# Routed experts on one core: the gathered rows of every second unit turned by VectorE from quarter rows, in place of four TensorE transposes

## The chip, the core and the metric

The kernel runs on one core of one Trainium2 chip. The metric is the time of the whole kernel in microseconds (us), less is better. Everything between the first load and the last store is in it.

## The reference, cut to what matters

The input `x` is 4 x 512 tokens of 512 numbers. A cross attention and a self attention (16 heads) are added to it; then comes the part that matters here, a mixture of 16 experts, six of which each token goes through:

```python
t = rmsnorm(x, ln2_w).reshape(-1, d)              # T = 2048 tokens, d = 512
probs = softmax(t @ gate_w.T)                      # E = 16 experts
topv, topi = top_k(probs, 6); topv = topv / sum(topv)
cw = zeros((T, E)).at[arange(T)[:, None], topi].add(topv)
g = einsum('td,eid->eti', t, eg_w)                 # I = 352
u = einsum('td,eid->eti', t, eu_w)
routed = einsum('eti,edi,te->td', silu(g) * u, ed_w, cw)
shared = silu(t @ sg_w.T) * (t @ su_w.T) @ sd_w.T
out = x + routed + shared
```

All is in fp32. A product of two fp32 matrices is made of three matmuls on parts (`matmul3`: high x high, high x low, low x high), where the high part is the number cut to the type fp32r and the low part is what is left.

## The kernel before, in words

The program is a chain of blocks: cross attention, self attention (beside it GpSimd splits all expert weights into high and low parts and stores them in memory), the second normalization, the shared expert with the routing tables, and last `routed_experts`, which the change is about.

The routing tables sort the (token, expert) pairs by expert and fill units of 128 lanes; there are `UNITS` = 111 units, whatever the routing. For each unit, `token_of[:, n]` has the 128 token numbers, `weight_of[:, n]` their weights; `expert_of` and `base_of` tell TensorE which expert it is and where its weights lie in the ring. The normalized rows lie in memory as `rows` (T + 128 rows of 512 numbers, 2 KB each; the last 128 are spare, for empty lanes).

What is done for a unit n, by engine (q = n % 2 chooses the buffer):

- GpSimd gathers the 128 rows of the unit into `xg[q]` by an indirect DMA (L1616), indexed by `gidx[q]`, which VectorE has copied from `token_of` (L1773). Later it scatters the unit's result `y[q]` with an add into the output (L1620). A scatter waits until the one before it has landed (semaphore `added`), because two of them may meet in one row. Before each of the two, a small instruction on `carry` (L1627) takes the waits. In its step m GpSimd issues the gather of unit m + 2 and the scatter of unit m - 3.
- TensorE transposes the gathered rows into `ps_x[q]` in four 128x128 transposes (`transposed`, L1664), ScalarE copies them out as the high part `xT[q][0]` (L1729), VectorE makes the low part (`low_rows`, L1754).
- TensorE makes the gate and the up product (`gate_up`, 24 matmuls of 352 columns, lines 67 to 69), ScalarE the silu (L1734), VectorE the product `prod` (L1767); TensorE transposes `prod` (`products`, L1697), ScalarE and VectorE split it into `hT` (L1738, L1775); TensorE makes the down product (`down`, 9 matmuls of 512 columns); VectorE weighs it into `y[q]` (`weigh`, L1762).

The order on each engine is written out by hand, in `step`; loops (`Fori`) run over pairs of units. TensorE's step n is: transposes of the rows of unit n + 2, register loads (`base`, `expert`), transposes of `prod` of unit n, gate and up product of unit n + 1, down product of unit n. VectorE's step n is: `prod` of n, `y` of n - 1, low part of the rows of n + 2, index copy for n + 4, `hT` low part of n. SyncE loads the weights of the experts into a ring of three slots, 16 pieces of 272 KB each (L1610), when the expert that had the slot is done.

Each engine waits with semaphores that count finished instructions: `pe_x` for the row transposes, `act_x` and `dve_x` for the copies, `dve_i` for the index copies, `ld_x` for the gathers. Here are `routed_experts` and what calls it:

Of the kernel before, what the change touches and what calls it, by code (L numbers as in the profile page):

```python
# [619 lines left out]
def routed_counters(sem):  # L620

    counters, count = counting(sem)
    for name in ("pool_c5", "pe_x", "act_x", "dve_x", "pe_g5", "pe_u5", "act_s5", "dve_p5", "pe_h5", "act_h5", "dve_h5",
                 "pe_d5", "dve_y", "dve_i"):
        count(name)
    return counters
# [939 lines left out]
def routed_experts(nc, sem, counters, ps, ident, token_of, weight_of, expert_of, base_of, ends_of, rows, ring, xg, ld_x, ld_ring,  # L1566
# [15 lines left out]
    with ExitStack() as ctx:  # L1582
# [10 lines left out]
        ps_g, ps_u, ps_x, ps_h, ps_d = ps[0], ps[1], ps[2:4], ps[4], ps[5:7]  # L1593

        pool_0 = sem("pool_05")
        (pool_c, pe_x, act_x, dve_x, pe_g, pe_u, act_s, dve_p, pe_h, act_h, dve_h, pe_d, dve_y, dve_i) = counters
# [16 lines left out]
        @block.gpsimd  # L1613
        def _(pool):
            def gather(q):
                nc.gpsimd.indirect_dma_start(xg[q][:, 0, :], None, rows, bass.IndirectOffsetOnAxis(ap=gidx[q][:], axis=0),  # L1616
                                             bounds_check=T + P - 1, oob_is_err=True).then_inc(ld_x[q], 16)

            def scatter(q):
                nc.gpsimd.indirect_dma_start(out, bass.IndirectOffsetOnAxis(ap=sidx[q][:], axis=0), y[q][:], None,  # L1620
                                             bounds_check=T + P - 1, oob_is_err=True,
                                             compute_op=ALU.add).then_inc(added, 16)

            def take_waits(done):
# [4 lines left out]
            def step(m, q, scatters=True, gathers=True):  # L1629

                if gathers:
                    pool.wait_ge(dve_i, ONE + m - 1)
                    pool.wait_ge(pe_x, ONE + m + 1)
                    take_waits(2 * m - 4)
                    gather(q)
                if scatters:
                    pool.wait_ge(dve_y, ONE + m - 2)
                    pool.wait_ge(added, FIRST + 16 * (m - 3))
                if gathers:
                    take_waits(2 * m - 3)  # L1640
                if scatters:
                    scatter(1 - q)

            nc.gpsimd.memset(carry[:], 0.0).then_inc(pool_0, 1)
            nc.gpsimd.memset(prod[:, I:NI * P], 0.0).then_inc(pool_0, 1)
            pool.wait_ge(pool_0, 2)
            pool.wait_ge(added, FIRST)
            for m in range(2, 4):
                if m == 3:
                    pool.wait_ge(stored, STORED)  # L1650
                step(m, m % 2, scatters=m > 2)
            with pool.Fori(2, TURNS + 1) as g:
                for q in range(2):
                    step(2 * g + q, q)
            for m in range(2 * TURNS + 2, UNITS + 3):
                step(m, m % 2, gathers=m + 2 < UNITS)
            pool.wait_ge(added, FIRST + 16 * UNITS)

        @block.tensor
        def _(pe):  # L1660
            def transposed(landed, q, half=0):
                pe.wait_ge(ld_x[q], 16 * landed)
                for j in range(DC):
                    last = nc.tensor.transpose(ps_x[q][:, j * P:(j + 1) * P], xg[q][:, half, j * P:(j + 1) * P], ident[:])  # L1664
                last.then_inc(pe_x, 1)

# [33 lines left out]
            def step(n, turn, q, half=0, rows=True, following=True, weighed=True):  # L1700
# [13 lines left out]
            gate_up(first, its_expert, 0, 0)  # L1714
            pe.wait_ge(pool_0, 2)
            for n in range(2):
                step(n, 0, n, half=1, weighed=False)
            with pe.Fori(1, TURNS + 1) as g:
                for q in range(2):
                    step(2 * g + q, g, q)  # L1720
            for n in range(2 * TURNS + 2, UNITS):
                step(n, n // 2, n % 2, rows=n + 2 < UNITS, following=n + 1 < UNITS)

        @block.scalar
        def _(act):
            def high_rows(n, q):

                act.wait_ge(pe_x, ONE + n + 1)
                nc.scalar.copy(xT[q][0][:], ps_x[q][:].rearrange("p (j t) -> p j t", j=DC)).then_inc(act_x, 1)  # L1729

            def step(n, q, more=True):
                act.wait_ge(pe_g, ONE + n + 1)
                act.wait_ge(dve_p, ONE + n)
                nc.scalar.activation(silu[:], ps_g[:, 0:I], ACT.Silu).then_inc(act_s, 1)  # L1734
                if more:
                    high_rows(n + 2, q)
                act.wait_ge(pe_h, ONE + n + 1)
                nc.scalar.copy(hT[0][:], ps_h[:, 0:NI * P].rearrange("p (c t) -> p c t", c=NI)).then_inc(act_h, 1)  # L1738

            for q in range(2):  # L1740
                high_rows(q, q)
            for n in range(2):
                step(n, n)
            with act.Fori(1, TURNS + 1) as g:
                for q in range(2):
                    step(2 * g + q, q)
            for n in range(2 * TURNS + 2, UNITS):
                step(n, n % 2, more=n + 2 < UNITS)

        @block.vector  # L1750
        def _(dve):
            def low_rows(n, q):
                dve.wait_ge(act_x, ONE + n + 1)
                nc.vector.tensor_tensor(xT[q][1][:], ps_x[q][:].rearrange("p (j t) -> p j t", j=DC),  # L1754
                                        xT[q][0][:].bitcast(F32), ALU.subtract).then_inc(dve_x, 1)
# [8 lines left out]
            def step(n, q, before=True, gathers=True, more=True):  # L1764
# [7 lines left out]
                if gathers:  # L1772
                    nc.vector.tensor_copy(gidx[q][:], token_of[:, bass.ds(n + 4, 1)]).then_inc(dve_i, 1)  # L1773
# [4 lines left out]
            dve.wait_ge(added, FIRST)  # L1778
            for q in range(2):
                low_rows(q, q)  # L1780
            for n in range(2):
                step(n, n, before=n > 0)
            with dve.Fori(1, TURNS) as g:
                for q in range(2):
                    step(2 * g + q, q)
            for n in range(2 * TURNS, UNITS):
                step(n, n % 2, gathers=n + 4 < UNITS, more=n + 2 < UNITS)
# [102 lines left out]
```

## Time and profile before

Three runs took 2204.24, 2204.88 and 2204.95 us, a median of 2204.88.

| what | value |
|---|---|
| profiled execution, its own time | 2203.29 us |
| its span, first to last instruction | 2201.4 us |
| PE (TensorE matmul) busy | 2122.8 us, 96% |
| DVE (VectorE) busy | 1145.1 us, 52% |
| POOL (GpSimd) busy | 962.9 us, 44% |
| ACT (ScalarE) busy | 720.7 us, 33% |
| mean granted TensorE clock | 0.987 of 2.4 GHz |
| DMA, mean over the span | 137 GB/s |
| routed stage | from about 1438 us to the end |

Times in the rows are in microseconds from the start of the span, unless they are marked ns. PEld is TensorE's weight load, which lies beside its matmuls. An engine's busy time leaves out register, branch and semaphore instructions. In a bracket behind a row stands how long the engine was idle before it and what released it; "issue" is idle time in which nothing that the profile shows was waited for. The time of a POOL DMA instruction is that in which GpSimd writes the descriptors; the data lands later.

### The profile page before, as it was taken

The numbers are of one execution on the slowest core, as the hardware profiler recorded it, in microseconds if no ns is written. First come the engines' busy times: TensorE is split into PE (matmuls) and PEld (weight loads), VectorE is DVE, ScalarE is ACT, GpSimd is POOL, SyncE is SP. The second block draws the span as 40 slices with busy tenths as digits, with TensorE's granted clock in tenths as the row PEclk, the third lists the DMA queues.
The fourth block names the chain that finished last, engine by engine and source line by source line (L and its number), as shares of the span: only waits on it lengthen the run. The fifth ranks groups of instructions, "written<-read, shape, count | busy, mean of one in ns | idle before, by whom it ended". The sixth has DMA issues, their size and how long they took to land. (4 is left out here: it accounts for less than half of the span.)

```text
span 2201.4 us, 39664 instructions
## 1 busy us (share of the span) xinstructions
PE 2122.8 (96%) x11850; PEld 1856.1 (84%) x11851; DVE 1145.1 (52%) x2520; ACT 720.7 (33%) x1896; POOL 962.9 (44%) x1004
## 2 busy tenths in 40 slices
PE   7899999999999999999996999989999999999996
PEld 6788888889888898888875777789999999999996
DVE  6746466464655646465666476633433333333332
ACT  6634344343434434343344222212222222222221
POOL 3545354545545454554515014434444444444442
PEclk9999999999999999999997999999999999999998
DMA  3214343443533344343416111186766766676443
GB/s 116 86 68 168 120 144 117 157 143 115 170 120 138 123 151 154 114 162 118 150 62 225 77 67 48 45 256 159 226 172 179 194 186 160 159 216 185 81 76 53
DMA packets 140690, 300.62 MB, mean 137 GB/s; under 512 B 16800, under 2 KB 16800, under 8 KB 138592
## 3 DMA queue, kind: packets, MB, share of 16 engines
q1 hardware_dynamic: 115392, 241.26, 31.0%
q0 software_dynamic: 24960, 58.21, 14.0%
q8 instruction: 27, 0.44, 0.1%
q10 hardware_dynamic: 288, 0.53, 0.1%
q14 instruction: 23, 0.19, 0.0%
HBM read 177.51 MB, written 122.42 MB: 136 GB/s over the span
## 5 line engine op out<-in xcount | busy, mean ns | idle before, releaser
L726 POOL TENSOR_TENSOR chunk_hi<-chunk_raw,zero 128x512 fp32r<-128x512 f32 x153 | 159.4, 1042 | 241.2 <-DMA chunk_raw<-in_whole 241.2
L1620 POOL DMA_INDIRECT out<-y,sidx x111 | 177.4, 1598 | 66.1 <-issue 44.4
L728 POOL TENSOR_TENSOR chunk_raw<-chunk_raw,chunk_hi 128x512 fp32r<-128x512 f32 x153 | 197.7, 1292 | 12.0
L936 DVE TENSOR_TENSOR pT_lo<-ps,pT_hi 128x384 fp32r<-128x384 f32 (+2 forms) x256 | 111.1, 455 | 176.6 <-ACT pT_hi L878 172.6
L1767 DVE TENSOR_TENSOR prod<-ps,silu 128x352 f32<-128x352 f32 x111 | 58.2, 524 | 271.0 <-PE ps L69 271.0
L909 DVE SCALAR_TENSOR_TENSOR HS<-ps,rinv,HS 128x512 f32<-128x512 f32 x260 | 176.6, 738 | 3.3 <-PE ps L69 3.3
L1627 POOL TENSOR_TENSOR carry<-ident 128x1 f32<-128x1 f32 x214 | 41.5, 194 | 295.9 <-DVE gidx L1773 209.6
L867 ACT ACTIVATE prob<-ps,negmax 128x512 f32<-128x512 f32 (+3 forms) x256 | 131.6, 527 | 110.0 <-DVE negmax L898 110.0
L1762 DVE TENSOR_SCALAR y<-ps,weight_of 128x512 f32<-128x512 f32 x111 | 83.3, 750 | 140.8 <-PE ps L69 140.7
L67 PE MATMUL ps<-ring,xT_0hi 128*128 x448 | 150.0, 335 | 0.8 <-DMA ring<-split_weights 0.8
L67 PE MATMUL ps<-wv_or_qk_hi,hT_hi 128*128 128x256 f32 x512 | 146.8, 287 | 2.9 <-PEq L134 2.9
L67 PE MATMUL ps<-ring,xT_1hi 128*128 x440 | 146.7, 333 | 0.0
L68 PE MATMUL ps<-wv_or_qk_lo,hT_hi 128*128 128x256 f32 x512 | 146.0, 285 | 0.0
L69 PE MATMUL ps<-wv_or_qk_hi,hT_lo 128*128 128x256 f32 x512 | 146.0, 285 | 0.0
L69 PE MATMUL ps<-ring,xT_0lo 128*128 x448 | 144.1, 322 | 0.0
L68 PE MATMUL ps<-ring,xT_0hi 128*128 x448 | 144.1, 322 | 0.0
L69 PE MATMUL ps<-ring,xT_1lo 128*128 x440 | 142.6, 324 | 0.0
L68 PE MATMUL ps<-ring,xT_1hi 128*128 x440 | 141.5, 322 | 0.0
L1616 POOL DMA_INDIRECT xg<-normed_rows,gidx x107 | 114.9, 1074 | 57.5 <-issue 36.7
L69 PE MATMUL ps<-ring,hT_lo 128*128 x333 | 131.4, 395 | 0.0
L67 PE MATMUL ps<-ring,hT_hi 128*128 x333 | 129.8, 390 | 1.4 <-DVE hT_lo L1775 1.4
L68 PE MATMUL ps<-ring,hT_hi 128*128 x333 | 131.1, 394 | 0.0
(322 smaller groups left out, 6002.1 us busy)
## 6 DMA issues: line engine op xcount, KB each, us to landing
ring<-split_weights SPq DMA_DIRECT2D x240, 272.0 KB, 6.8
chunk_raw<-in_whole SPq DMA_DIRECT2D x153, 256.0 KB, 2.7
split_weights<-chunk_hi SPq DMA_DIRECT2D x153, 256.0 KB, 2.4
split_weights<-chunk_raw SPq DMA_DIRECT2D x153, 256.0 KB, 2.6
xg<-in_wqk SPq DMA_DIRECT2D x16, 512.0 KB, 3.8
x_spill<-x SPq DMA_DIRECT2D x4, 1024.0 KB, 3.9
xg<-in_wv SPq DMA_DIRECT2D x8, 512.0 KB, 3.5
xg<-in_wo SPq DMA_DIRECT2D x8, 512.0 KB, 5.1
```

Source lines behind the costliest of these rows:

```text
L67: nc.tensor.matmul(out, lhs[0], rhs[0], start=start, stop=False)
L68: nc.tensor.matmul(out, lhs[0], rhs[1], start=False, stop=False)
L69: return nc.tensor.matmul(out, lhs[1], rhs[0], start=False, stop=stop)
L726: nc.gpsimd.tensor_tensor(chunk_hi[k][:], chunk_raw[k][:], zero[:].to_broadcast([P, CH]), ALU.add).then_inc(chunk_high, 1)
L728: nc.gpsimd.tensor_tensor(chunk_raw[k][:].bitcast(F32R), chunk_raw[k][:], chunk_hi[k][:].bitcast(F32), ALU.subtract).then_inc(chunk_low, 1)
L867: nc.scalar.activation(prob[i][:], ps_s[i][:, 0:(i + 1) * P], ACT.Exp, bias=negmax[:, s % 2, i:i + 1], accum_out=rsum[:, s % 2, i:i + 1]). ...
L909: nc.vector.scalar_tensor_tensor(out=hs, in0=ps_w[i][:], scalar=rinv[:, (s - 1) % 2, i:i + 1], in1=hs, op0=ALU.mult, op1=ALU.add).then_inc ...
L936: nc.vector.tensor_tensor(pT[1][:, 0:split, w], ps_t[k % 2][:, 0:split * P].rearrange("p (j t) -> p j t", t=P), pT[0][:, 0:split, w].bitca ...
L1616: nc.gpsimd.indirect_dma_start(xg[q][:, 0, :], None, rows, bass.IndirectOffsetOnAxis(ap=gidx[q][:], axis=0), bounds_check=T + P - 1, oob_i ...
L1620: nc.gpsimd.indirect_dma_start(out, bass.IndirectOffsetOnAxis(ap=sidx[q][:], axis=0), y[q][:], None, bounds_check=T + P - 1, oob_is_err=Tr ...
L1762: nc.vector.tensor_scalar(y[q][:], ps_d[q][:], weight_of[:, bass.ds(n, 1)], None, ALU.mult).then_inc(dve_y, 1)
L1767: nc.vector.tensor_tensor(prod[:, 0:I], ps_u[:, 0:I], silu[:], ALU.mult).then_inc(dve_p, 1)
```

## The change

Units 5, 7, ... 109 (odd, from the fifth on) get their transposed rows in another way. The transpose on VectorE turns each block of 32x32 in its place. So GpSimd gathers quarter rows, of 512 bytes: partition 32a + j gets, for t = 0 to 3, the quarter a of the row of lane 32t + j. These are four indirect DMAs of 128 quarter rows each, in place of one of 128 rows. Then one VectorE transpose of 128x512 from `xg[1]` (which it reads with a step of four elements) into `ps_x[1]` gives the turned rows. The indices of the quarters, `quarter_of` = 4 x token + a, are made once, at the stage's start, by four small fp32 matmuls on TensorE that spread the token numbers over the partitions and one VectorE instruction; ScalarE makes the operands of these matmuls.

With that the order of the 512 features over chunk and partition becomes (partition, chunk) in place of (chunk, partition), for all units and the experts' gate and up weights; the host lays out the weights so, and TensorE's transposes that are left read `xg` with a step of four elements. TensorE's step of an odd unit has no row transposes any more; its register loads are made ahead of the last chunk of the down product before it. ScalarE's and VectorE's copies out of `ps_x` have the same number of elements in another order. VectorE's turn for the rows of unit n + 2 stands first in its step n, and GpSimd may gather into `xg[1]` again when the turn is done (`dve_turned`).

```diff
-        gidx = [sb(f"gidx{q}", [P, 1], U32) for q in range(2)]
+        gidx = [sb(f"gidx{q}", [P, 1 + 3 * q], U32) for q in range(2)]
+        tokens = sb("tokens5", [P, UNITS])
+        lanes = sb("lanes5", [P, 4, P])
+        group = sb("group5", [P, 1])
+        quarter_of = sb("quarter_of", [P, UNITS, 4], U32)
...
+        quarters = rows.rearrange("r (a n) -> (r a) n", a=4)
...
+        turned_rows = lambda q: [ps_x[0][:].rearrange("p (c t j) -> p t c j", c=DC, t=4),
+                                 ps_x[1][:].rearrange("p (t c j) -> p t c j", t=4, c=DC)][q]
+        of_parts = lambda x: x[:].rearrange("p c (t j) -> p t c j", t=4)
...
             def gather(q):
-                nc.gpsimd.indirect_dma_start(xg[q][:, 0, :], None, rows, bass.IndirectOffsetOnAxis(ap=gidx[q][:], axis=0),
-                                             bounds_check=T + P - 1, oob_is_err=True).then_inc(ld_x[q], 16)
+                if q == 0:
+                    nc.gpsimd.indirect_dma_start(xg[0][:, 0, :], None, rows, bass.IndirectOffsetOnAxis(ap=gidx[0][:], axis=0),
+                                                 bounds_check=T + P - 1, oob_is_err=True).then_inc(ld_x[0], 16)
+                    return
+                for t in range(4):
+                    nc.gpsimd.indirect_dma_start(xg[1][:, 0, t * P:(t + 1) * P], None, quarters,
+                                                 bass.IndirectOffsetOnAxis(ap=gidx[1][:, t:t + 1], axis=0),
+                                                 bounds_check=4 * (T + P) - 1, oob_is_err=True).then_inc(ld_x[1], 16)
...
                 if gathers:
                     pool.wait_ge(dve_i, ONE + m - 1)
-                    pool.wait_ge(pe_x, ONE + m + 1)
+                    if m < 4:
+                        pool.wait_ge(pe_x, ONE + m + 1)
+                    elif q == 0:
+                        pool.wait_ge(pe_x, ONE + turn + 3)
+                    else:
+                        pool.wait_ge(dve_turned, ONE + turn - 1)
                     take_waits(2 * m - 4)
                     gather(q)
                 if scatters:
...
             def transposed(landed, q, half=0):
                 pe.wait_ge(ld_x[q], 16 * landed)
-                for j in range(DC):
-                    last = nc.tensor.transpose(ps_x[q][:, j * P:(j + 1) * P], xg[q][:, half, j * P:(j + 1) * P], ident[:])
+                by_tile = xg[q][:, half, :].rearrange("p (m c) -> p c m", c=DC)
+                for c in range(DC):
+                    last = nc.tensor.transpose(ps_x[q][:, c * P:(c + 1) * P], by_tile[:, c], ident[:])
                 last.then_inc(pe_x, 1)
+            def token_quarters():
+                pe.wait_ge(act_tokens, 2)
+                for t in range(4):
+                    last = nc.tensor.matmul(ps_q[:, t * UNITS:(t + 1) * UNITS], lanes[:, t, :], tokens[:], start=True, stop=True)
+                last.then_inc(pe_tokens, 1)
...
-            def down(at, n, q, weighed=True):
+            def down(at, n, q, weighed=True, between=None):
                 if weighed:
                     pe.wait_ge(dve_y, ONE + n - 1)
                 pe.wait_ge(dve_h, ONE + n + 1)
+                found = None
                 for c in range(NI):
+                    if between and c == NI - 1:
+                        found = between()
                     last = matmul3(nc, ps_d[q][:], [h[:, c, :] for h in hT], weights(at, GU + c * D, D), c == 0, c == NI - 1)
                 last.then_inc(pe_d, 1)
+                return found
...
+            def places(n, following=True):
+                return (base(n), base(n + 1), expert(n + 1)) if following else (base(n),)
+            def step(n, turn, q, half=0, rows=True, following=True, weighed=True, found=None, between=None):
                 if rows:
                     transposed(turn + 2, q, half)
-                own = base(n)
-                if following:
-                    at, its_expert = base(n + 1), expert(n + 1)
+                own, *after = found or places(n, following)
                 products(n)
                 if following:
-                    gate_up(at, its_expert, n + 1, 1 - q)
-                down(own, n, q, weighed)
+                    gate_up(*after, n + 1, 1 - q)
+                return down(own, n, q, weighed, between)
...
+            token_quarters()
             pe.wait_ge(pool_0, 2)
             for n in range(2):
                 step(n, 0, n, half=1, weighed=False)
             with pe.Fori(1, TURNS + 1) as g:
-                for q in range(2):
-                    step(2 * g + q, g, q)
+                found = step(2 * g, g, 0, between=lambda: places(2 * g + 1))
+                step(2 * g + 1, g, 1, rows=False, found=found)
             for n in range(2 * TURNS + 2, UNITS):
-                step(n, n // 2, n % 2, rows=n + 2 < UNITS, following=n + 1 < UNITS)
+                step(n, n // 2, n % 2, rows=n % 2 == 0 and n + 2 < UNITS, following=n + 1 < UNITS)
...
+            def high_rows(n, turn, q):
+                if n < 4:
+                    act.wait_ge(pe_x, ONE + n + 1)
+                    nc.scalar.copy(xT[q][0][:], ps_x[q][:].rearrange("p (j t) -> p j t", j=DC)).then_inc(act_x, 1)
+                    return
+                if q == 0:
+                    act.wait_ge(pe_x, ONE + turn + 3)
+                else:
+                    act.wait_ge(dve_turned, ONE + turn - 1)
+                    act.wait_ge(pe_u, ONE + n - 1)
+                nc.scalar.copy(of_parts(xT[q][0]), turned_rows(q)).then_inc(act_x, 1)
...
+            nc.scalar.copy(tokens[:], token_of[:]).then_inc(act_tokens, 1)
+            nc.scalar.copy(lanes[:].rearrange("p t (a j) -> p t a j", a=4),
+                           ident[:].rearrange("p (t j) -> p t j", t=4).unsqueeze(2).to_broadcast([P, 4, 4, 32])).then_inc(act_tokens, 1)
...
+            def turn_rows(n, turn):
+                dve.wait_ge(ld_x[1], 32 + 64 * (turn - 1))
+                dve.wait_ge(act_x, ONE + n - 1)
+                dve.wait_ge(dve_x, ONE + n - 1)
+                nc.vector.transpose(ps_x[1][:].rearrange("p (t c j) -> p t c j", t=4, c=DC),
+                                    xg[1][:, 0, :].rearrange("p (t i c) -> p t c i", t=4, c=DC)).then_inc(dve_turned, 1)
...
+            def step(n, turn, q, before=True, gathers=True, more=True):
+                if q and more and n >= 2:
+                    turn_rows(n + 2, turn + 1)
                 dve.wait_ge(act_s, ONE + n + 1)
                 dve.wait_ge(pe_u, ONE + n + 1)
                 nc.vector.tensor_tensor(prod[:, 0:I], ps_u[:, 0:I], silu[:], ALU.mult).then_inc(dve_p, 1)
...
                 if more:
                     low_rows(n + 2, q)
                 if gathers:
-                    nc.vector.tensor_copy(gidx[q][:], token_of[:, bass.ds(n + 4, 1)]).then_inc(dve_i, 1)
+                    if q == 0:
+                        nc.vector.tensor_copy(gidx[0][:], token_of[:, bass.ds(n + 4, 1)]).then_inc(dve_i, 1)
+                    else:
+                        nc.vector.tensor_copy(gidx[1][:], quarter_of[:, bass.ds(n + 4, 1), :].rearrange("p u t -> p (u t)")).then_inc(dve_i, 1)
...
+            for a in range(4):
+                nc.vector.memset(group[32 * a:32 * a + 32, :], float(a)).then_inc(dve_quarters, 1)
             for q in range(2):
                 low_rows(q, q)
+            dve.wait_ge(dve_quarters, 4)
+            dve.wait_ge(pe_tokens, 1)
+            nc.vector.tensor_scalar(quarter_of[:].rearrange("p u t -> p t u"),
+                                    ps_q[:, 0:4 * UNITS].rearrange("p (t u) -> p t u", t=4), 4.0, group[:, 0:1],
+                                    ALU.mult, ALU.add).then_inc(dve_quarters, 1)
+            dve.wait_ge(dve_quarters, 5)
...
-    gu = gu.transpose(0, 1, 3, 2).reshape(NE, 2, DC, P, I).transpose(3, 0, 1, 2, 4).reshape(P, NE, GU)
+    gu = gu.transpose(0, 1, 3, 2).reshape(NE, 2, P, DC, I).transpose(2, 0, 1, 3, 4).reshape(P, NE, GU)
```

## Rows read from the trace of the kernel before

**Rows 1.** One stretch: length; busy PE, PEld, DVE, ACT, POOL; clock, DMA share, GB/s

```profile
1450.00:1700.00 250.00, 250.00 (x1496) 233.68 (x1496) 96.28 (x224) 53.27 (x112) 113.09 (x150) 1.00 0.71 187
```

**Rows 2.** TensorE in order of time, two units (start, duration, x count)

```profile
1600.39 0.39 PE L69 MATMUL ps<-ring,hT_lo 128*128 x1
...
1607.05 0.39 PE L69 MATMUL ps<-ring,hT_lo 128*128 x1
1607.28 0.60 PE L1664 MATMUL ps<-ident,xg 128*128 128x128 f32 x4
1607.71 0.49 PE L1697 MATMUL ps<-ident,prod 128*128 128x128 f32 x3
...
1613.76 0.39 PE L69 MATMUL ps<-ring,hT_lo 128*128 x1
```

**Rows 3.** GpSimd in order of time where it is behind

```profile
1641.64 1.60 POOL L1620 DMA_INDIRECT out<-y,sidx  x1 [0.58 <-issue]
...
1643.71 1.08 POOL L1616 DMA_INDIRECT xg<-normed_rows,gidx  x1 [0.24 <-issue]
1646.58 0.19 POOL L1627 TENSOR_TENSOR carry<-ident 128x1 f32<-128x1 f32 x1 [1.79 <-DMA out<-y,sidx]
1647.43 1.60 POOL L1620 DMA_INDIRECT out<-y,sidx  x1 [0.66 <-issue]
```

**Rows 4.** instructions of L1616, then of L1620: issue to landing

```profile
DMA to landing us min/median/max: 3.3/3.5/7.4
DMA to landing us min/median/max: 4.7/4.9/8.7
```

**Rows 5.** scatters at the first and the last of 14 long intervals

```profile
1457.80 1.64 POOL L1620 DMA_INDIRECT out<-y,sidx  x1 [0.17 <-issue]
...
1467.12 1.59 POOL L1620 DMA_INDIRECT out<-y,sidx  x1 [0.59 <-issue]
...
1473.24 1.59 POOL L1620 DMA_INDIRECT out<-y,sidx  x1 [0.92 <-issue]
...
2019.63 1.60 POOL L1620 DMA_INDIRECT out<-y,sidx  x1 [0.17 <-issue]
...
2029.19 1.60 POOL L1620 DMA_INDIRECT out<-y,sidx  x1 [0.58 <-issue]
```

**Rows 6.** VectorE and GpSimd in order of time, one unit

```profile
1609.14 0.14 DVE L1773 COPY gidx<-token_of 128x1 uint32 x1
1609.20 0.55 DVE L1775 TENSOR_TENSOR hT_lo<-ps,hT_hi 128x384 fp32r<-128x384 f32 x1
1610.26 1.07 POOL L1616 DMA_INDIRECT xg<-normed_rows,gidx  x1 [0.53 <-issue]
...
1612.18 0.53 DVE L1767 TENSOR_TENSOR prod<-ps,silu 128x352 f32<-128x352 f32 x1 [2.43 <-PE ps L69]
...
1614.28 0.75 DVE L1762 TENSOR_SCALAR y<-ps,weight_of 128x512 f32<-128x512 f32 x1 [1.52 <-PE ps L69]
```

**Rows 7.** GpSimd's gathers ahead of the routed stage, two of four

```profile
1429.79 1.01 POOL L1260 DMA_INDIRECT xg<-normed_rows,token_of  x1 [0.30 <-issue]
1431.10 1.01 POOL L1260 DMA_INDIRECT xg<-normed_rows,token_of  x1 [0.30 <-issue]
```

**Rows 8.** GpSimd in order of time, a gather and a scatter

```profile
1616.96 1.08 POOL L1616 DMA_INDIRECT xg<-normed_rows,gidx  x1 [0.52 <-issue]
...
1618.43 1.60 POOL L1620 DMA_INDIRECT out<-y,sidx  x1 [0.17 <-issue]
```

**Rows 9.** L1257's duration; packets of three L1257, one L1616, one L1620

```profile
L1257 POOL DMA_DIRECT2D begin<-ident x3: 549/582/833, 1421.4 to 1422.8; - x3
...
q0 software_dynamic: 96, 0.00, 0.9%
...
q0 software_dynamic: 81, 0.26, 20.7%
...
q0 software_dynamic: 145, 0.26, 60.0%
```

More of the change, by code:

```diff
@@ L1627, in take_waits, with step @@
                 nc.gpsimd.tensor_tensor(carry[:], ident[:, 0:1], ident[:, 0:1], ALU.add).then_inc(pool_c, 1)
-            def step(m, q, scatters=True, gathers=True):
+            def step(m, turn, q, scatters=True, gathers=True):
                 if gathers:
                     pool.wait_ge(dve_i, ONE + m - 1)
-                    pool.wait_ge(pe_x, ONE + m + 1)
+                    if m < 4:
[4 more added lines that the diff above has]
+                        pool.wait_ge(dve_turned, ONE + turn - 1)
                     take_waits(2 * m - 4)
@@ L1650, in _ @@
                     pool.wait_ge(stored, STORED)
-                step(m, m % 2, scatters=m > 2)
+                step(m, 1, m % 2, scatters=m > 2)
             with pool.Fori(2, TURNS + 1) as g:
                 for q in range(2):
-                    step(2 * g + q, q)
+                    step(2 * g + q, g, q)
             for m in range(2 * TURNS + 2, UNITS + 3):
-                step(m, m % 2, gathers=m + 2 < UNITS)
+                step(m, m // 2, m % 2, gathers=m + 2 < UNITS)
             pool.wait_ge(added, FIRST + 16 * UNITS)
@@ L1718, in _, with step @@
             with pe.Fori(1, TURNS + 1) as g:
-                for q in range(2):
-                    step(2 * g + q, g, q)
+                found = step(2 * g, g, 0, between=lambda: places(2 * g + 1))
+                step(2 * g + 1, g, 1, rows=False, found=found)
             for n in range(2 * TURNS + 2, UNITS):
-                step(n, n // 2, n % 2, rows=n + 2 < UNITS, following=n + 1 < UNITS)
+                step(n, n // 2, n % 2, rows=n % 2 == 0 and n + 2 < UNITS, following=n + 1 < UNITS)
         @block.scalar
         def _(act):
[L1726 to L1731, printed above, removed]
+            def high_rows(n, turn, q):
[9 more added lines that the diff above has]
+                nc.scalar.copy(of_parts(xT[q][0]), turned_rows(q)).then_inc(act_x, 1)
+            def step(n, turn, q, more=True):
                 act.wait_ge(pe_g, ONE + n + 1)
@@ L1735, in step @@
                 if more:
[L1736 removed]
+                    high_rows(n + 2, turn + 1, q)
                 act.wait_ge(pe_h, ONE + n + 1)
                 nc.scalar.copy(hT[0][:], ps_h[:, 0:NI * P].rearrange("p (c t) -> p c t", c=NI)).then_inc(act_h, 1)
+            nc.scalar.copy(tokens[:], token_of[:]).then_inc(act_tokens, 1)
+            nc.scalar.copy(lanes[:].rearrange("p t (a j) -> p t a j", a=4),
+                           ident[:].rearrange("p (t j) -> p t j", t=4).unsqueeze(2).to_broadcast([P, 4, 4, 32])).then_inc(act_tokens, 1)
             for q in range(2):
[L1741 removed]
+                high_rows(q, 0, q)
             for n in range(2):
[L1743 removed]
+                step(n, 0, n)
             with act.Fori(1, TURNS + 1) as g:
                 for q in range(2):
[L1746 removed]
+                    step(2 * g + q, g, q)
             for n in range(2 * TURNS + 2, UNITS):
[L1748 removed]
+                step(n, n // 2, n % 2, more=n + 2 < UNITS)
         @block.vector
         def _(dve):
+            def turn_rows(n, turn):
[4 more added lines that the diff above has]
+                                    xg[1][:, 0, :].rearrange("p (t i c) -> p t c i", t=4, c=DC)).then_inc(dve_turned, 1)
             def low_rows(n, q):
                 dve.wait_ge(act_x, ONE + n + 1)
[L1754 to L1755 removed]
+                if n < 4:
+                    nc.vector.tensor_tensor(xT[q][1][:], ps_x[q][:].rearrange("p (j t) -> p j t", j=DC),
+                                            xT[q][0][:].bitcast(F32), ALU.subtract).then_inc(dve_x, 1)
+                    return
+                nc.vector.tensor_tensor(of_parts(xT[q][1]), turned_rows(q), of_parts(xT[q][0]).bitcast(F32),
+                                        ALU.subtract).then_inc(dve_x, 1)
             def weigh(n, q):
@@ L1778, in _ @@
             dve.wait_ge(added, FIRST)
+            for a in range(4):
+                nc.vector.memset(group[32 * a:32 * a + 32, :], float(a)).then_inc(dve_quarters, 1)
             for q in range(2):
                 low_rows(q, q)
+            dve.wait_ge(dve_quarters, 4)
[4 more added lines that the diff above has]
+            dve.wait_ge(dve_quarters, 5)
             for n in range(2):
-                step(n, n, before=n > 0)
+                step(n, 0, n, before=n > 0)
             with dve.Fori(1, TURNS) as g:
                 for q in range(2):
-                    step(2 * g + q, q)
+                    step(2 * g + q, g, q)
             for n in range(2 * TURNS, UNITS):
-                step(n, n % 2, gathers=n + 4 < UNITS, more=n + 2 < UNITS)
+                step(n, n // 2, n % 2, gathers=n + 4 < UNITS, more=n + 2 < UNITS)
             weigh(UNITS - 1, (UNITS - 1) % 2)
```

10 lines of the change are left out of this document (5 added, 5 removed).

## The prediction

> **What bounds the kernel now.** I read the stage rows first, then TensorE's, VectorE's and GpSimd's instructions of two units in order of time. In the routed stage TensorE is busy in all of 250 us, at the full granted clock of 1.00 (the 2.4 GHz level), while VectorE has 96 us of work in them, GpSimd 113, and the DMA engines are busy 71% [rows 1]. So the routed stage is TensorE's, and everything else is cover. From the last matmul of one unit's down product (1600.39) to that of the unit two later (1613.76) it is 13.37 us, without a gap. The four transposes of the gathered rows start at 1607.28 and the next ones, of the gate-up product, at 1607.71: 0.43 us per unit [rows 2].
>
> The reader should then look at what runs close behind. GpSimd does a gather and a scatter for each unit, and each scatter waits until the scatter before it has landed. Where GpSimd is behind, the chain is seen bare: scatter at 1641.64, landed (the small `carry` instruction is released) at 1646.58, next scatter at 1647.43. That is 5.79 us from scatter to scatter, against the 6.69 us that TensorE takes for a unit, with one gather inside it for nothing [rows 3]. While the next expert's weights are loaded, a scatter takes up to 8.7 us to land in place of 4.9, a gather 7.4 in place of 3.5 [rows 4]; the interval becomes 9.32 to 9.56 us, in each of 14 places, of which the first and the last are shown, and the one after the first is 6.12 [rows 5]. Today GpSimd has 0.9 us per unit to make that up.
>
> **What is removed.** 111 units, of which 5, 7, ... 109 (53) lose four TensorE transposes: 53 x 0.43 = 22.8 us if TensorE stays the bound; the pair then takes 12.94 us. The three register loads of those steps move ahead of the last chunk of the down product, which is three matmuls of 0.23 us; in the old place four transposes (0.43 us) hid them without a gap [rows 2], so I cost the move at nothing, and at 0.1 to 0.4 us per pair if the cover fails.
>
> **VectorE and ScalarE.** One turn of 128x512 per pair. The trace has no such instruction; the nearest rows are 128x512 from or to PSUM, 0.75 us, and 128x384, 0.55 [rows 6]. I take 0.75, and let it be twice that. It stands ahead of `prod`, where VectorE now idles 2.43 us [rows 6], so it costs nothing if its rows are there. ScalarE's copy of these rows starts earlier than today and is not late for anything. If the rows are not there, `prod`, and TensorE's transposes of `prod`, wait with it: that is the new wait of this change, and `y`, `low_rows`, the index copy and `hT_lo` stand behind it on VectorE.
>
> **GpSimd.** Three more indirect DMAs per pair, in the same queue as the scatters. Four gathers without waits between them are in the trace, before the routed stage: 1.01 us each, 1.31 from one start to the next [rows 7]. Bounds: 1.08 and the 0.52 us of dispatch after a wait, 1.60 [rows 3, 8], from above; from below 0.58 us, a plain DMA of 4 bytes per partition (0.88 with its gap). The packets speak for something low: such a plain DMA has 32 packets (96 for three), a gather 80 or 81 and takes 1.08, a scatter 144 or 145 and takes 1.60 [rows 3, 9]; that is 8 ns a packet, and a quarter-row gather, if its four packets' worth of bytes is 16 data packets of 4 KB, would have 32 and take 0.68. But the number of rows stays 128, and a scatter also adds, so packets and work can't be told apart here; I take 1.31, the only row of the same operation in the same sequence. [...]
>
> The pair's chain on GpSimd in quiet stretches, with everything ready: from the scatter after four gathers to the scatter after one, 5.79 (landing bound, the one gather hides). From there to the next one: scatter to gather 2.07 [rows 3], three more gathers 3 x 1.31 = 3.93, last gather to scatter 1.47 [rows 8], sum 7.47. Together 13.26 us per pair. That is more than TensorE's new 12.94 and nearly its old 13.37. So GpSimd becomes the bound, and in quiet stretches the gain is 0.11 us per pair: 52 x 0.11 = 5.7 us. How TensorE comes to wait: the quarter rows of a unit are asked for right after the index copy; first gather 0.98 us later [rows 6], last one 3.93 after that, landed 3.5 later, which is 8.4 us. The copy ends at 1609.28 [rows 6]; two steps on, TensorE wants `prod` at 1613.76 + 0.23 + 6.69 - 0.43 = 1620.25, 11.0 us later; less 0.53 for `prod`, 0.75 for the turn and 0.3 for handing over, the rows must be there 9.4 us after the copy. That is one microsecond of slack, used up in three pairs or by the first load.
>
> **The weight loads.** With no slack left, each slow landing is lost for good. In the half with one gather the interval goes from 5.79 to 9.32 or 9.56: 3.65. In the half with four it goes from 7.47 to the same 9.4 (2.0), and the next interval of 6.12 is 0.33 over 5.79: 2.3. The mean is 3.0, times 14 is 42 us.
>
> **The start.** Four small fp32 matmuls behind the first gate-up product, and one VectorE instruction of 444 columns ahead of the first `prod`, both on the path once: between 4 x 0.11 and 1.7 us and about 0.7 us (the 0.75 row); I take 1.4 us. The memsets, the token copy and the lane copy lie where ScalarE and VectorE wait for the first rows.
>
> **Sum.** -5.7 + 42 + 1.4 - 1.0 (the slack) = +36.7 us. The profiled execution took 2203.3 us (span 2201.4), 1.6 under the median of the runs, 2204.9; I add to the median: 2241.6, said as 2241.
>
> **Rivals.**
> A, the forecast above: GpSimd's chain of waits bounds the stage. 50%.
> B, the gather's instruction costs by its packets, pitch 0.98 in place of 1.31. The second half of the chain is 2.07 + 2.94 + 1.07 = 6.08, the pair 11.87, under 12.94: TensorE stays the bound, and 22.8 us come off. Slow landings then have 1.07 us per pair to be made up in, so what they cost is between nothing (2183.5 with the start) and some 1.6 us each (the last quarter gather is issued 0.98 + 2.94 after the copy and lands 6.5 later, 10.4 against 9.4, and 0.6 for GpSimd's own lateness), 22 us (2206); the middle is 2195. For it: the packet counts. Against it: [rows 7]. It decides from a pitch of about 1.2 downward. 35%, three quarters of it on the faster side.
> C, the four gathers of a loop have the long dispatch, pitch 1.60: 0.87 more per pair than A, 45 us, 2287. Against it: 0.52 is seen only behind a wait. 10%.
> D, the strided reads. TensorE's remaining transposes and the turn read every fourth element, 16 bytes apart; no row here shows such a read. If it doubled the transposes' 0.43 us, the pair's TensorE time would be 13.37 again, as before: with cheap gathers no gain and the loads' stalls, 2206 to 2228. 5%. The Trainium skill, page SBUF — State Buffer, section Door 1: The DMA port swizzle, has 16-byte lines in SBUF and a penalty for each access that crosses to a new one, which every one of these does. By that rule D would hold, though under A it would change the time little, for 13.37 is only 0.11 over GpSimd's 13.26.
>
> That the change doesn't do what it says would need the turned rows to be transposed on TensorE as well; the diff leaves no such call.
>
> **How the numbers follow.** No change is what lies within 0.2%, 4.4 us, about what a measurement of this kernel can tell. Faster than 2200.5: three quarters of B and a few per cent of A with a low pitch, 0.30. Within: the rest of B, 0.09. Slower: 0.61. The likeliest case alone ranges from 2222 (loads at 2 us each, pitch 1.27) to 2262 (4 us each, pitch 1.38). The 8-in-10 range reaches into B and towards C: 2187 to 2272.
>
> **What would show it.** Right: 58 instead of 111 groups of row transposes, TensorE with idle time ahead of the transposes of `prod` and a released-by VectorE or DMA beside it, GpSimd hardly idle except for landings, scatter intervals alternating near 5.8 and 7.5, a pitch of 1.3 between quarter gathers, and pairs of 13.3 us in quiet stretches, 16 where a load runs. Wrong, towards B: quarter gathers of 0.7 us, pairs of 12.94 us with TensorE busy throughout. Wrong, towards D: a pitch over 0.11 us between the transposes that are left. A turn well over 1.5 us, or four quarters that land much later than 3.5 us behind the last issue (the order of small packets among the weights' large ones), would make A's price per load too low.

## The result, and the profile after

The change makes the kernel slower: 2251.41 us, median of 4 runs (2247.86 to 2251.88), against 2204.91 for the kernel before (2204.24 to 2209.71), a ratio of 1.0203 with a 95% interval of 1.0185 to 1.0220. The forecast was 2241 us, in the range 2187 to 2272. The profiled execution took 2251.63 us, span 2249.9, 48.5 us more than the span before.

The first view is the same stretch of the routed stage as [rows 1] (length; busy PE, PEld, DVE, ACT, POOL; granted clock, DMA share, GB/s).

```profile
1450.00:1700.00 250.00, 229.94 (x1317) 209.41 (x1318) 105.51 (x224) 52.40 (x105) 153.53 (x184) 1.00 0.67 182
```

TensorE, which was never idle there, is idle for 20 us at the same full clock, with 179 instructions fewer, the removed transposes among them. GpSimd has gone from 113 to 154 us. What GpSimd, VectorE and TensorE wait for is in the waits between 1450 and 2200 us (engine, line, releaser: us in total, times, longest):

```profile
DVE sidx L1821 <- DMA out<-y,sidx: 225.3, 101, 6.1
...
POOL carry L1645 <- DMA out<-y,sidx: 148.6, 57, 6.4
...
DVE ps L1806 <- DMA xg<-normed_rows,gidx: 78.4, 47, 4.1
...
POOL xg L1633 <- issue: 56.8, 197, 1.5
...
PEld ps L67 <- issue: 48.6, 53, 2.2
...
PE ps L67 <- DVE hT_lo L1841: 15.4, 19, 1.9
PE ps L67 <- issue: 14.5, 13, 1.5
```

GpSimd's waits for a scatter to land come once per pair (57 for 52 pairs and the ends), and VectorE waits for the same landing before it may overwrite the scatter's indices (`sidx`), 101 times. In the kernel before, that wait was met 30 times and cost 24.9 us. One quiet pair on GpSimd, in order of time:

```profile
1700.48 1.64 POOL L1638 DMA_INDIRECT out<-y,sidx  x1 [0.16 <-issue]
...
1702.49 1.07 POOL L1629 DMA_INDIRECT xg<-normed_rows,gidx  x1 [0.15 <-issue]
1705.42 0.18 POOL L1645 TENSOR_TENSOR carry<-ident 128x1 f32<-128x1 f32 x1 [1.86 <-DMA out<-y,sidx]
1706.19 1.59 POOL L1638 DMA_INDIRECT out<-y,sidx  x1 [0.59 <-issue]
...
1708.16 1.06 POOL L1633 DMA_INDIRECT xg<-normed_rows,gidx  x1 [0.15 <-issue]
1709.53 1.01 POOL L1633 DMA_INDIRECT xg<-normed_rows,gidx  x1 [0.30 <-issue]
...
1712.16 1.01 POOL L1633 DMA_INDIRECT xg<-normed_rows,gidx  x1 [0.30 <-issue]
...
1713.56 1.63 POOL L1638 DMA_INDIRECT out<-y,sidx  x1 [0.16 <-issue]
```

The half with one gather takes 5.71 us and ends on a landing; the half with four takes 7.37 and ends on no wait at all, for the landing of 1706.19 is long past when the fourth gather is out. Together 13.08; over the 32 pairs of under 14 us the mean is 13.21.

**The whole difference by stretches of scatters.** The first scatter comes 8.1 us later (1465.9 against 1457.8). The 52 pairs from there take 743.0 us against 695.6, +47.4. The six scatters after them take 3.2 less and the rest of the program 3.8 less. Together +48.5. The +47.4 splits into 52 x 13.21 against 52 x 13.38, -8.7, and 56.1 us by which the other pairs, above all those in which the weights of experts 3 to 15 are loaded, are longer than a quiet one. These are 13 loads: the one for expert 2, which made the first long interval of the kernel before (9.32 us at 1457.80), is issued between 1454.3 and 1462.9 and lies ahead of the first scatter here.

### The profile page after: what moved, and what is told of

It is laid out like the page before. It is cut to its first block and busy times, and to the rows that moved or that the text cites. A ratio compares the mean times of both kernels' runs of the same rounds, so it can differ in the third digit from the quotient of the medians.

```text
span 2249.9 us, 39793 instructions
## 1 busy us (share of the span) xinstructions
PE 2121.1 (94%) x11646; PEld 1836.2 (82%) x11647; DVE 1199.1 (53%) x2578; ACT 727.9 (32%) x1898; POOL 1127.6 (50%) x1163
## 5 line engine op out<-in xcount | busy, mean ns | idle before, releaser
L1633 POOL DMA_INDIRECT xg<-normed_rows,gidx x212 | 217.5, 1026 | 61.2 <-issue 57.6
L1645 POOL TENSOR_TENSOR carry<-ident 128x1 f32<-128x1 f32 x214 | 89.4, 418 | 171.0 <-DMA out<-y,sidx 150.4
L67 PE MATMUL ps<-ring,hT_hi 128*128 x333 | 135.7, 408 | 31.4 <-DVE hT_lo L1841 16.7
L1821 DVE COPY sidx<-token_of 128x1 uint32 (+1 forms) x111 | 17.1, 154 | 231.3 <-DMA out<-y,sidx 231.2
L719 POOL TENSOR_TENSOR wv_or_qk_hi<-xg,zero 128x1024 fp32r<-128x1024 f32 x15 | 28.4, 1892 | 209.7 <-PE ps L69 209.7
L68 PE MATMUL ps<-ring,hT_hi 128*128 x333 | 130.8, 393 | 0.0
```

Source lines behind the costliest of these rows:

```text
L67: nc.tensor.matmul(out, lhs[0], rhs[0], start=start, stop=False)
L68: nc.tensor.matmul(out, lhs[0], rhs[1], start=False, stop=False)
L719: nc.gpsimd.tensor_tensor(dst[0], raw[r], zero[:].to_broadcast([P, 1024]), ALU.add).then_inc(pool_hi, 1)
L1633: nc.gpsimd.indirect_dma_start(xg[1][:, 0, t * P:(t + 1) * P], None, quarters, bass.IndirectOffsetOnAxis(ap=gidx[1][:, t:t + 1], axis=0), ...
```

## The experiments

**Is it the count of gathers?** `one_of_four` sends one quarter gather per odd unit in place of four (and so leaves out three quarters of those rows); `before_plus3` adds three quarter gathers per odd unit, into a spare tile, to the kernel before, whose TensorE then waits until all four have landed; nothing else of its work is changed.

```
one_of_four:   for t in range(1):   # was range(4);  turn_rows waits for 32 + 16 * (turn - 1)
before_plus3:  for t in range(3 * q):
                   nc.gpsimd.indirect_dma_start(spare_rows[:, t * P:(t + 1) * P], None, quarters, ...)
```

> The changed kernel with one quarter gather per odd unit in place of four; the other three quarters of those rows are left out, so the turned rows hold old data. Theory 1 (GpSimd's chain of issue and landing bounds the stage): the half with four gathers shrinks from 7.38 us to one that is bound by a landing, 5.8, the pair to 11.6, under TensorE's 12.92, so TensorE is the bound again: 2184 to 2205 us. Theory 2 (what costs is on VectorE and TensorE: the turn of 1.10 us ahead of prod, the reads of every fourth element, the moved register loads): all of that is still there, so 2235 us or more.

> The kernel before with three quarter gathers more per odd unit, into a spare tile; TensorE waits for all four DMAs. Nothing of the turn is in it. Theory 1: GpSimd's pair is 13.2 us in quiet stretches, just under TensorE's 13.37, and each of 14 weight loads costs it about 4 us of which little is made up; some 5 us of slack are used up once: 2235 to 2255 us. Theory 2: extra gathers cost nothing, 2205 us.

Measured: 2187.15 us (2185.90 to 2189.85), 0.9925 [0.9911, 0.9940]; and 2254.38 (2253.82 to 2256.15), 1.0230 [1.0215, 1.0245]. The second has TensorE's transposes, no turn and no strided read, and is as slow as the change. Its GpSimd:

```profile
1662.97 1.07 POOL L1618 DMA_INDIRECT xg<-normed_rows,gidx  x1 [0.15 <-issue]
1664.35 1.02 POOL L1621 DMA_INDIRECT spare_rows<-normed_rows,gidx  x1 [0.30 <-issue]
...
1666.98 1.01 POOL L1621 DMA_INDIRECT spare_rows<-normed_rows,gidx  x1 [0.30 <-issue]
...
1668.38 1.64 POOL L1626 DMA_INDIRECT out<-y,sidx  x1 [0.16 <-issue]
...
1673.92 1.59 POOL L1626 DMA_INDIRECT out<-y,sidx  x1 [0.58 <-issue]
```

The half with one gather is 5.54 us here, and the mean quiet pair is 13.23, as in the change (13.21). So the three gathers and the wait for them, without the turn, make the loss; with them there, taking the transposes from TensorE is worth about 3 us, which is not clear of noise (2254.4 to 2251.4; the intervals of the two ratios overlap), and without them 17.3 us.

**What do the weight loads add?** `after_small` cuts the loads of experts 3 to 15 to 4 columns per piece.

```
width = PIECE if e < SLOTS else 4
sp.dma_start(ring[:, at:at + width].bitcast(F32), split_w[half][:, source:source + width])
```

> The changed kernel with the weight loads of experts 3 to 15 cut to 4 columns of each of their 16 pieces, so these experts compute with the weights of earlier ones. Theory 1 (two parts: GpSimd's quiet pair of 13.2 us, a little under the old 13.37, and some 4 us lost per weight load): without the loads only the first part and the start are left, 2195 to 2203 us. Theory 4 (most of the loss is in the quiet pairs and the start, loads were hidden as before): 2235 us or more.

Measured: 2202.89 us (2199.86 to 2206.21), 0.9994 [0.9985, 1.0004]. The 52 pairs take 695.5 us in place of 743.0: the 13 loads cost 47.5 us, 3.7 each. The quiet pairs stay at 13.17.

**Is it the size of the load or its burst?** `after_paced` is the change with the same bytes, two pieces at a time: before every second piece SP waits until the pieces issued so far have landed. `before_paced` is the same edit in the kernel before.

```
nth = half * PIECES + k
if nth and nth % 2 == 0:
    sp.wait_ge(ld_ring, LOADED + PER_EXPERT * (e - 1) + 16 * nth)
```

> The changed kernel, all of it computed, with each expert's 16 pieces loaded two at a time, the next two only when the first have landed, so that a load is spread out and takes the DMA engines less fully. Theory 1: landings of scatters and gathers in a load are less slow, but there are more of them; if the queue in front of a scatter's packets is what makes it slow, about half of the 56 us comes back: 2215 to 2235 us. If only the bytes count, nothing comes back: 2250.

> Control: the kernel before with the same pacing. Its scatters have slack, so no change by either theory, 2204 us, unless an expert's weights come too late for TensorE, which would show as a wait for the ring.

Measured: 2218.32 us (2215.42 to 2225.97), 1.0059 [1.0042, 1.0076]; and 2203.99 (2202.64 to 2207.12), 0.9999 [0.9990, 1.0009]. A load unpaced in the change, on GpSimd, ahead of the fence above; the scatter before these rows started at 1682.08:

```profile
1691.00 0.19 POOL L1645 TENSOR_TENSOR carry<-ident 128x1 f32<-128x1 f32 x1 [5.84 <-DMA out<-y,sidx]
1691.76 1.60 POOL L1638 DMA_INDIRECT out<-y,sidx  x1 [0.58 <-issue]
...
1695.07 1.07 POOL L1633 DMA_INDIRECT xg<-normed_rows,gidx  x1 [1.48 <-issue]
```

That scatter took 8.9 us to land, and the interval is 9.68. The next one is 8.72, because the four gathers start 1.3 us late; that part is not the load's doing. The 32nd and the 94th scatter have this late start in the change, in `after_paced` and in `after_small` alike, and in `after_small` no weights of normal size are on their way:

```profile
1674.05 1.60 POOL L1639 DMA_INDIRECT out<-y,sidx  x1 [0.58 <-issue]
...
1677.36 1.07 POOL L1634 DMA_INDIRECT xg<-normed_rows,gidx  x1 [1.48 <-issue]
```

What holds these two gathers is open. In `after_paced` the 52 pairs take 714.6 us in place of 743.0, with quiet pairs of 13.35; its profiled execution, 2225.97 us, was the slowest of its four. The same bytes spread out cost 28 us less; where GpSimd has slack, in the kernel before, it makes no difference.

**Can the chain of landings be opened?** `two_outputs` scatters the odd units into a buffer of their own, counted by a semaphore of their own (it leaves out the sum of the two buffers).

```
out_of = [out, nc.dram_tensor("out_odd", [T + P, D], F32, kind="Internal").ap()]
nc.gpsimd.indirect_dma_start(out_of[q], ...).then_inc(added_of[q], 16)
pool.wait_ge(added_of[1 - q], before_of[1 - q] + 16 * (turn - 2 + q))
```

> The changed kernel with the odd units scattered into a buffer of their own with a semaphore of their own, so a scatter waits for the landing of the one two before; the sum of the two buffers is left out, so the output lacks the odd units. Theory 1: the landing wait is what makes the single half 5.8 us and a load cost 4 us. Without it GpSimd's pair is 7.38 + 3.5 = 10.9 us of issue, TensorE is the bound: 2188 to 2210 us. Theory 3 (GpSimd's own work of four gathers is too much, landing or not): still over 2235 us.

Measured: 2229.41 us (2226.49 to 2234.03), 1.0110 [1.0095, 1.0125]: a miss by 19 us. The chain did open, and another wait took over:

```profile
2017.27 1.63 POOL L1643 DMA_INDIRECT out<-y,sidx  x1 [0.16 <-issue]
...
2020.74 1.60 POOL L1643 DMA_INDIRECT out_odd<-y,sidx  x1 [0.17 <-issue]
2023.86 0.18 POOL L1650 TENSOR_TENSOR carry<-ident 128x1 f32<-128x1 f32 x1 [1.52 <-DVE gidx L1846]
...
2029.98 1.64 POOL L1643 DMA_INDIRECT out<-y,sidx  x1 [0.16 <-issue]
```

Intervals of 3.47 and 9.24 us; GpSimd now waits for the odd unit's index copy, and the quiet pair, 12.94 in the median, is TensorE's 12.92. The loads still stall it, by intervals of 11.3 to 13.2 us: the quarter rows land late, and the turn stands ahead of `prod`, so `prod` and TensorE wait for a gather. I had priced the loads on the landings of scatters alone.

**A version that keeps the turn.** Two parts. GpSimd's: two quarter gathers ahead of each of the pair's scatters, so that both halves are alike. VectorE's: the turn behind `prod` and `hT_lo`, no longer ahead of them, and `hT` ahead of the turned rows on ScalarE. `split` has both, `order_only` and `pool_split_only` one each, and `split_paced` has both with the paced loads, and the token matmuls ahead of the first gate-up product.

```
GpSimd's:   if q == 0 and m >= 4: gather(1, range(2, 4))    # behind the even unit's gather
            gather(q, range(2))
VectorE's:  prod(n); weigh(n - 1); low_of_products(n); turn_rows(n + 2, turn + 1); gidx copy; low_rows(n + 2, q)
```

> The changed kernel, all of it computed, with two quarter gathers of an odd unit ahead of one scatter and the other two ahead of the next, where GpSimd waits for a landing anyway; the turn stands behind y and hT_lo on VectorE, and ScalarE copies hT ahead of the turned rows. Theory 1: halves of 5.8 (landing) and 2.07 + 2 x 1.32 + 1.47 = 6.2 us, the pair 12.0, under 12.92; TensorE is the bound, and a load is made up in three pairs: 2188 to 2205 us, faster than before if the start doesn't eat it. Theory 2 or 3: no faster than 2240 us.

> The changed kernel with only the order on VectorE and ScalarE of the split kernel (hT_lo, then the turn, then the index copy, behind y; hT copied ahead of the turned rows), the four gathers together as in the change. Theory 1: GpSimd's chain of four gathers, a scatter, a landing and one gather is untouched, 13.2 us a pair and 3.5 to 4 us a load, so nothing changes: 2245 to 2255 us. Theory 2 (the turn ahead of prod is what costs): 2215 us or less.

> The changed kernel with only GpSimd's part of the split kernel, two quarter gathers ahead of each scatter, the turn still ahead of prod. GpSimd's chain is 12.2 us a pair, but the last quarter is issued 0.98 + 1.33 + 1.47 + 2.07 + 1.33 = 7.2 us after the index copy and lands 3.5 later, 10.7 against a limit of about 9.1 with a turn of 1.10 us. From index copy to index copy over landing, turn, prod and y the loop is then about 14 us a pair: 2230 to 2260 us. If the turn's place doesn't matter: 2213 us as the split kernel.

> The split kernel (two quarter gathers ahead of each scatter, the turn later on VectorE) with the pacing, and with the four token matmuls ahead of the first gate-up product, where TensorE waits for its weights. Theory 1: quiet pairs of 12.92 us, loads that cost less than the 2.5 to 3.5 us each that they cost in the split kernel, and 1 to 1.5 us less at the start: 2186 to 2202 us, faster than both kernels. If pacing brings nothing: 2211 us.

| kernel | median us (range) | ratio, 95% | 52 pairs, us |
|---|---|---|---|
| `order_only` | 2278.33 (2276.12 to 2279.79) | 1.0335 [1.0317, 1.0352] | 767.8 |
| the change | 2251.41 | 1.0203 [1.0185, 1.0220] | 743.0 |
| `pool_split_only` | 2248.57 (2245.84 to 2249.17) | 1.0198 [1.0181, 1.0215] | 741.6 |
| `split` | 2213.23 (2212.05 to 2220.43) | 1.0046 [1.0034, 1.0058] | 706.6 |
| `split_paced` | 2182.21 (2181.52 to 2184.81) | 0.9902 [0.9886, 0.9919] | 677.9 |

`order_only` missed by 23 us, and its GpSimd and VectorE show why:

```profile
1712.49 0.15 DVE L1824 COPY sidx<-token_of 128x1 uint32 x1 [2.63 <-DMA out<-y,sidx]
...
1713.31 1.59 POOL L1638 DMA_INDIRECT out<-y,sidx  x1 [0.58 <-issue]
...
1713.75 1.10 DVE L1809 STREAM_TRANSPOSE ps<-xg 128x512 f32<-128x512 f32 x1
1714.76 0.15 DVE L1844 COPY gidx<-quarter_of 128x4 uint32 x1
1715.18 0.18 POOL L1645 TENSOR_TENSOR carry<-ident 128x1 f32<-128x1 f32 x1 [0.28 <-DVE gidx L1844]
1715.89 1.07 POOL L1633 DMA_INDIRECT xg<-normed_rows,gidx  x1 [0.53 <-issue]
```

VectorE runs in order. The copy of the next gather's indices stands behind `sidx`, which waits for a landing. In the change only `y` and the low part of the rows (0.68 us) lie between the two; here `y`, `hT_lo` and the turn of 1.10 us do. So the first quarter gather starts 2.58 us after the scatter, in place of 1.97 in the change, the quiet pair is 13.81 in place of 13.21, 52 x 0.60 = 31 us more; 6 us less at the loads leave the 25 us between the two sums. `pool_split_only` is 2.8 us below the change, which is not clear of noise: with two gathers in each half its quiet pair is the same 13.17, and its turn, still ahead of `prod`, waits 158.9 us for rows. Its granted clock is 0.97 between 1500 and 2100 us, where the change and `split` have 1.00; how much of its time that is, was not tried. Together the two parts gain 38 us (2251.4 to 2213.2), 8 us short of the range expected: the loads still made 21 intervals of 8.4 to 9.35 us. Pacing them took 28.7 us off the 52 pairs, and the first scatter comes 2.0 us earlier (1460.2 in place of 1462.2). That goes with the moved token matmuls: pacing alone moved it from 1457.8 to 1457.6 in the kernel before and from 1465.9 to 1468.0 in the change. GpSimd in one pair of `split_paced`, and its stretch as in [rows 1]:

```profile
1885.33 1.63 POOL L1641 DMA_INDIRECT out<-y,sidx  x1 [0.16 <-issue]
...
1888.86 1.07 POOL L1636 DMA_INDIRECT xg<-normed_rows,gidx  x1 [0.53 <-issue]
1890.23 1.01 POOL L1636 DMA_INDIRECT xg<-normed_rows,gidx  x1 [0.31 <-issue]
...
1892.42 1.63 POOL L1641 DMA_INDIRECT out<-y,sidx  x1 [0.58 <-issue]
...
1898.67 1.61 POOL L1641 DMA_INDIRECT out<-y,sidx  x1 [0.32 <-issue]
```

```profile
1450.00:1700.00 250.00, 249.31 (x1462) 232.04 (x1461) 119.09 (x246) 55.61 (x115) 172.05 (x206) 1.00 0.79 198
```

TensorE is busy again in all but 0.7 of 250 us, its pair is 12.97 in the median, and the kernel, which computes everything, is 21.6 us faster than the one before, of 22.8 that the removed transposes were worth.

## Why the prediction was right

Case A was right in its mechanism, and 10 us low, 2251.4 for 2241. Part of the closeness is luck, for the start was short by 6.7 us and the end, not counted at all, gave back 7.0. By its steps:

- **What is removed.** 22.8 us if TensorE stays the bound. TensorE's pair, where it waits for nothing, is 12.92 (predicted 12.94); `one_of_four` and `split_paced` bring 17.3 and 21.6 us.
- **The quarter gathers.** 212 of them at 1.01 us and a pitch of 1.31 to 1.38, as taken; the packets did not lead to B, and the dispatch between them was 0.30, not C's 0.52. GpSimd's time for a gather of 128 rows did not go with the row length: in sequence one of 512-byte rows takes 1.01 us, as one of 2 KB rows did [rows 7], and the first behind a scatter takes 1.07 with either length.
- **The quiet pair.** Predicted 5.79 + 7.47 = 13.26, measured 13.21; the term -5.7 was -8.7 us.
- **The loads, the term that was mis-sized.** Predicted 3.0 us each for 14, 42. `after_small` gives 47.5 us for the 13 that fall into the 52 pairs, 3.7 each; the excess over quiet pairs is 56.1, and 10.7 of excess are left in `after_small`. I had read 9.32 to 9.56 for the long intervals of the kernel before in each of 14 places; they are 8.70 to 9.74, 9.39 in the mean, so that reading did not mis-size it. Per half I took 3.65 or 2.3. Where the load met the half with one gather (eight times) it cost 3.6 to 5.0 us (intervals of 9.35 to 10.8). Where it met the half with four first (five times) I had 2.3, from an interval of 9.4 and a nearly quiet one of 6.12 behind it. Measured are 8.5 to 8.7 and then 8.4 to 8.6, 3.9 to 4.2 us over 5.79 + 7.38, because the landing behind the stalled half is slow as well:

```profile
1875.85 1.59 POOL L1638 DMA_INDIRECT out<-y,sidx  x1 [0.58 <-issue]
...
1884.51 1.62 POOL L1638 DMA_INDIRECT out<-y,sidx  x1 [0.58 <-issue]
...
1892.27 0.18 POOL L1645 TENSOR_TENSOR carry<-ident 128x1 f32<-128x1 f32 x1 [4.70 <-DMA out<-y,sidx]
1893.04 1.60 POOL L1638 DMA_INDIRECT out<-y,sidx  x1 [0.58 <-issue]
```

- **The slack.** 1.0 us was to be saved; it can't be read apart from the excess of the first pairs, so whether it came is open.
- **The start.** Predicted 1.4. The first scatter is 8.1 us late: the stage starts 1.6 later, and `prod` of the first unit starts at 1450.66 in place of 1446.56. Of the 2.5 us beyond that, 1.9 are the small matmuls' and the index arithmetic's, and 0.6 the clock's: the first gate-up product takes 5.9 us in place of 5.3, with a granted clock of 0.50 from 1440 to 1445 us and 0.81 from 1445 to 1450, where the kernel before has 0.60 and 1.00. The remaining 4.0 are the four gathers that now precede the first scatter (1460.5 to 1465.9), which I did not count as an item of the start; in `one_of_four` the first scatter comes at 1461.7. At the end 7.0 us come back, also uncounted: 3.2 over the last six scatters, with no gathers between them, and 3.8 behind the last one, where GpSimd's closing DRAIN takes 3.49 us in place of 7.17, for a cause that is open.

```profile
1448.47 1.04 PE L1695 MATMUL ps<-tokens,lanes 128*128 128x111 f32 x8
...
1449.62 1.01 DVE L1851 TENSOR_SCALAR quarter_of<-ps,group 128x444 uint32<-128x444 f32 x1 [6.42 <-PE ps L1695]
...
1450.66 0.53 DVE L1830 TENSOR_TENSOR prod<-ps,silu 128x352 f32<-128x352 f32 x1
```

- **The turn and the strided reads.** Durations are ns, min/median/max:

```profile
L1806 DVE STREAM_TRANSPOSE ps<-xg x53: 1081/1098/1121, 1470.1 to 2210.2; 128x512 f32<-128x512 f32 x53
...
L1688 PEld LDWEIGHTS ps<-ident,xg x232: 195/207/226, 1439.9 to 2219.9; 128*128 128x128 f32 x116
...
L305 PEld LDWEIGHTS ps<-ident,xg x32: 138/140/142, 62.1 to 89.8; 128*128 128x128 f32 x32
```

The turn takes 1.10 us, in place of 0.75, within its bound of 1.5; whether the strided read or the operation itself makes the difference, no run tells. TensorE's remaining transposes load every fourth element as weights in 207 ns where contiguous ones take 140, but the four pass in 0.47 us, from the first to the second of these rows, in place of 0.43 [rows 2].

```profile
1711.13 0.63 PE L1688 MATMUL ps<-ident,xg 128*128 128x128 f32 x4
1711.60 0.49 PE L1732 MATMUL ps<-ident,prod 128*128 128x128 f32 x3
```

So D, which wanted 0.43 us more, was wrong by a factor of ten. The Trainium skill, SBUF — State Buffer, Door 1: The DMA port swizzle, has a penalty for each access that goes to a new 16-byte line; the trace shows a dearer load, and nearly all of it is hidden.

- **The moved register loads.** Costed at nothing, or 0.1 to 0.4 us where the cover fails. It fails in 13 places, by more:

```profile
1702.24 0.40 PE L69 MATMUL ps<-ring,hT_lo 128*128 x1
1704.11 0.49 PE L67 MATMUL ps<-ring,hT_hi 128*128 x1 [1.48 <-issue]
```

Here it moved no end: `y` starts at 1705.51, right behind `sidx`, which a landing released at 1705.38. `split_paced` has the loads in the same place and TensorE without such a gap. But where the landing is early, the gap counts, as in `after_small`, whose seven long pairs make the 10.7 us of excess named above. In four of the seven, TensorE stands still for 1.00 to 1.17 us in this place; `y` is late by it, the index copy behind `y` too, and GpSimd waits 1.1 to 1.7 us for the copy, in intervals of 8.84 to 9.45 where 7.38 is quiet:

```profile
1511.89 0.49 PE L67 MATMUL ps<-ring,hT_hi 128*128 x1 [1.00 <-issue]
...
1512.97 0.75 DVE L1824 TENSOR_SCALAR y<-ps,weight_of 128x512 f32<-128x512 f32 x1 [1.75 <-PE ps L69]
...
1514.24 0.16 DVE L1840 COPY gidx<-quarter_of 128x4 uint32 x1
...
1514.59 0.18 POOL L1646 TENSOR_TENSOR carry<-ident 128x1 f32<-128x1 f32 x1 [1.12 <-DVE gidx L1840]
```

Two more of the seven are the late gathers of the 32nd and the 94th scatter, and in the last GpSimd waits for the index copy as well. That the moved loads make the gap is argued from its place alone, since the profile gives no releaser but "issue"; no run had them back in the old place.

- **A wait not named.** I followed the landing into GpSimd alone. VectorE waits for it too (225.3 us), and behind that wait stand `y` and the next indices. In the quiet pairs of the change it costs nothing of its own, since GpSimd waits for the same event; in the load at 1637.48 it adds 1.1 us, for the next scatter (1648.26) waits 1.68 us for the index copy where 0.58 is usual, and the interval is 10.77; it is what broke `order_only`.

## What to carry to other kernels

Work taken from the bounding engine is worth what the next chain of waits leaves of it: write out that chain's time per round with the added instructions in it, here 13.26 against 12.94 us, before counting the gain. On an in-order engine, look at what each moved instruction now stands ahead of; of the two edits one gained at most 3 us alone and the other lost 27, and together they gained 38. And where small transfers that others wait for run beside a bulk load with no slack, try spreading the load first: here it gave 33 us, and 31 together with the moved token matmuls.

## What was not expected of the hardware

The time of a small scatter beside a bulk load hangs on how the bulk transfers are issued, not on their bytes alone. With two pieces of a weight load at a time, one interval of `split_paced` is over 8.2 us (8.56), where `split` has 21. The pacing took 33 us off the change and nothing off the kernel before, with the same bytes moved. Whether the number of pieces on their way does it or the lower rate at which they are issued is not told apart, and other counts than two at a time were not tried.
